# Causal maxima masked on VectorE, products made in sets, and a new order for all engines: a two-attention, expert-FFN kernel on one Trainium2 core

## What is computed

```python
_OFFSETS = list(range(41)) + [128, 96, 384]
idx = jnp.arange(T)[:, None] - deltas[None, :]        # A: each row looks at 44 earlier rows
k_mod = k_g * (1.0 + scale_embed)
scores = jnp.einsum('bhtd,bhtjd->bhtj', q, k_mod) * scale
scores = scores + pos_bias.T[None, :, None, :]
scores = jnp.where(valid[None, None], scores, jnp.finfo(scores.dtype).min)
attn = jax.nn.softmax(scores, axis=-1)
...
scores = jnp.einsum('bhqd,bhkd->bhqk', Q, K) / jnp.sqrt(jnp.float32(D_HEAD))   # B: causal attention
scores = jnp.where(causal, scores, -jnp.inf)
...
h = jax.nn.relu(jnp.einsum('nm,emh->enh', cont, We1) + be1[:, None, :])        # F: 8 experts, top 2
...
x = x + A(_layernorm(x)); x = x + F(_layernorm(x)); x = x + B(_layernorm(x)); x = x + F(_layernorm(x))
```

## Time and profile before

| | before |
|---|---|
| median of 3 runs | 1962.25 us (1960.55 to 1966.32) |
| the profiled execution: its time, its span | 1972.26 us, 1970.2 us |
| mean granted TensorE clock | 0.949 of full speed |
| busy PE, DVE, ACT, POOL | 1745.7, 1297.8, 804.7, 119.0 us |

### The profile page before, as it was taken

How to read it: one execution, slowest core, us unless ns; L and a number is a source line. 1 busy time by engine, 2 the same in 40 slices (tenths; PEclk the granted TensorE clock), 3 DMA queues, 4 the chain that set the end, 5 groups by cost and what they waited for, 6 DMA issues and landing times.

```text
span 1970.2 us, 29536 instructions
## 1 busy us (share of the span) xinstructions
PE 1745.7 (89%) x11263; PEld 918.3 (47%) x11312; DVE 1297.8 (66%) x3090; ACT 804.7 (41%) x1473; POOL 119.0 (6%) x155
## 2 busy tenths in 40 slices
PE   5588888899999899998999999998999899998976
PEld 2163454345453555436453455435554345454443
DVE  6939764785659756686659757696566964745433
ACT  1123425234453445434462434533454253452623
POOL 1010110001000100002000010001000010000000
PEclk9779988999999999999999999999999999998989
DMA  8220250014200250005200240003400023104000
GB/s 287 90 73 23 98 172 3 23 70 144 58 24 23 105 165 3 24 22 204 67 23 23 81 167 23 24 23 138 132 24 1 23 105 127 50 2 129 3 11 11
DMA packets 47842, 137.91 MB, mean 70 GB/s; under 512 B 6184, under 2 KB 18856, under 8 KB 42920
## 3 DMA queue, kind: packets, MB, share of 16 engines
q1 hardware_dynamic: 47704, 136.02, 21.1%
HBM read 80.79 MB, written 46.04 MB: 64 GB/s over the span
## 4 chain that ended last, share of the span: by engine, by line
PE 59%; DVE 28%; issue 5%; ACT 3%; DMA 3%; POOL 0%; SPq 0%; POOLq 0%; DVEq 0%; ACTq 0%
PE bank L1435 22%; DVE arena_AB L1216 15%; PE bank L1703 6%; PE bank L1718 5%; DVE arena_AB L1272 4%; PE bank L1606 4%; PE bank L1625 3%; PE bank L1523 3%; PE bank L1537 2%; PE bank L1590 2%; PE bank L1558 2%; PE bank L1456 2%; PE bank L1443 1%; PE bank L1608 1%; DMA arena_AB<-stacks 1%
## 5 line engine op out<-in xcount | busy, mean ns | idle before, releaser
L1216 DVE TENSOR_TENSOR arena_AB<-qT,kT 128x512 f32<-128x512 f32 x704 | 428.4, 683 | 8.6 <-ACT kT L971 7.6
L1435 PE MATMUL bank<-arena_F,kept 128*128 128x512 f32 (+1 forms) x544 | 265.3, 615 | 15.8 <-ACT cont_hi L1059 4.2
L1523 PE MATMUL bank<-arena_AB,slot_w 128*32 128x512 f32 x1408 | 212.4, 643 | 54.9 <-DVE arena_AB L1216 52.9
L1272 DVE TENSOR_REDUCE arena_AB<-bank 128x1 f32<-128x512 f32 (+3 forms) x512 | 214.5, 481 | 67.6 <-PE bank L1592 66.0
L1069 ACT ACTIVATE arena_F<-bank,kept 128x512 f32<-128x512 f32 x256 | 169.0, 691 | 152.0 <-PE bank L1435 149.6
L1034 ACT ACTIVATE arena_AB<-bank 128x512 f32<-128x512 f32 (+1 forms) x352 | 178.7, 577 | 105.9 <-PE bank L1608 105.6
L1435 PEld LDWEIGHTS bank<-arena_F,kept 128*128 128x128 f32 (+1 forms) x544 | 93.6, 190 | 124.0 <-issue 99.2
L1590 PE MATMUL bank<-arena_AB 96*128 96x512 bf16 (+3 forms) x512 | 132.9, 317 | 10.0 <-ACT arena_F L1069 3.3
L1606 PE MATMUL bank<-arena_AB 99*128 99x256 bf16 (+3 forms) x512 | 127.3, 305 | 3.2 <-DMA arena_AB<-maxima 3.0
L1703 PE MATMUL bank<-arena_F,kept 128*64 128x512 f32 x512 | 126.0, 613 | 3.0 <-issue 1.9
L1435 PE MATMUL bank<-xnT,kept 128*128 128x512 f32 x256 | 125.7, 630 | 2.1 <-ACT xnT L953 1.7
(11 more groups left out here) (192 smaller groups left out, 2493.7 us busy)
## 6 DMA issues: line engine op xcount, KB each, us to landing
arena_AB<-band SPq DMA_DIRECT2D x32, 1344.0 KB, 6.3
arena_AB<-stacks SPq DMA_DIRECT2D x64, 384.0 KB, 8.4
stacks<-arena_AB SPq DMA_DIRECT2D x48, 256.0 KB, 2.9
band<-arena_AB SPq DMA_DIRECT2D x32, 328.0 KB, 2.2
stacks<-xnT SPq DMA_DIRECT2D x32, 256.0 KB, 2.6
band<-kT SPq DMA_DIRECT2D x4, 1352.0 KB, 21.8
v<-V SPq DMA_DIRECT2D x8, 576.0 KB
stacks<-xn SPq DMA_DIRECT2D x16, 256.0 KB, 3.1
```

Source lines behind the costliest of these rows:

```text
L1216: nc.vector.tensor_tensor(prod[n % RD], qT[:, hf, :], kT[:, hf, at:at + T], ALU.mult).then_inc(sem["A"]["prod_made"], 1)
L1272: ins = nc.vector.tensor_reduce(neg_max[:, n, i:i + 1], ps[:, at:at + (i + 1) * P], AX, ALU.max, negate=True)
L1435: ins = nc.tensor.matmul(out(ps), w, x, start=n == 0, stop=n == len(pairs) - 1)
L1523: ins = nc.tensor.matmul(ps[HS * col:HS * (col + 1), :], slot_w[:, slot(n), :], prod[n % RD], start=False, stop=r == 3, skip_group_check=True)
```

## The change

Six edits.
1. B's maxima: the mask matmul L1592 is gone. VectorE takes the minimum of the negated masked scores in one call, `tensor_tensor_reduce`, which reads the scores in PSUM and a bf16 mask in SBUF, writes the scores' place in PSUM and gives the row value.
2. A's products: up to four offsets that lie 4 rows apart come from one instruction of 128x2048; the far offsets stay single. The ring of products holds 4 sets in place of 18 products.
3. A's `ahead` matmul moves from the front of a group to its end and covers 40, 24 or 384 columns in place of 512.
4. A's `oT`: the 16 matmuls of 128 keys stand first, and then the 16 of 40 keys.
5. Values are stored 17 columns a head and not 32.
6. The scheduler's lengths are new, each block's end has a delay after it, and a block on PE that changes the array's mode costs 0.1 more. The table has some 70 lengths; two lines of it are shown.

```diff
-        p.put(("S", h, n), ("PE", (0.3, 0.45, 0.25)[n], ("stack", h // 4, "DMA")), ("DVE", (0.62, 0.8, 0.36)[n]))
+        p.put(("S", h, n), ("PE", (0.22, 0.23, 0.12)[n], ("stack", h // 4, "DMA")), ("DVE", (0.62, 0.76, 0.37)[n]))
...
-            p.put(("oT", i), ("PE", 2.0, *needs), ("ACT", 0.55))
+            p.put(("oT", i), ("PE", 1.35 if i > 0 else 0.86, *needs), ("ACT", 0.48))
...
+AFTER = {"PE": 0.2, "DVE": 0.13, "ACT": 0.16, "POOL": 0.1, "SP": 0.0, "DMA": 0.0}
+LOAD = 0.1
...
+def tiled(u, phase):
+    kind = phase[0] if isinstance(phase, tuple) else phase
+    return kind in ("prod", "PV", "eo") or u.stage == "A" and kind == "oT"
...
-                if e != "DMA":
+                if e == "PE":
+                    t = max(t + LOAD, free[e] + (LOAD if tiled(u, x[1]) != last_tiled else 0.0))
+                elif e != "DMA":
                     t = max(t, free[e])
...
-            done[x] = t + blocks[x]
+        done[x] = t + blocks[x] + AFTER[e]
...
-        v_96 = sb("v_96", [P, TT, H, HS])
+        v_96 = sb("v_96", [P, TT, H * HV])
...
-                        for n in SETS[i]:
-                            at = PAD - SLOTS[slot(n)]
-                            if n >= RD:
-                                dve.wait_ge(*product_used(u, n - RD))
-                            nc.vector.tensor_tensor(prod[n % RD], qT[:, hf, :], kT[:, hf, at:at + T], ALU.mult
-                                                    ).then_inc(sem["A"]["prod_made"], 1)
+                        if i >= RQ:
+                            dve.wait_ge(*products_used(u, i - RQ))
+                        for run in runs(i):
+                            col, at, c = PRODUCTS[run[0]][2], PAD - SLOTS[slot(run[0])], len(run)
+                            k = kT[:, hf, at:at + T]
+                            k = bass.AP(k.tensor, k.offset, [k.ap[0], [4, c], [1, T]])
+                            ins = nc.vector.tensor_tensor(prod[i % RQ][:, col:col + c, :],
+                                                          qT[:, hf, :].unsqueeze(1).broadcast_to([P, c, T]), k, ALU.mult)
+                        ins.then_inc(sem["A"]["prod_made"], 1)
...
-                            ins = nc.vector.tensor_reduce(neg_max[:, n, i:i + 1], ps[:, at:at + (i + 1) * P], AX,
-                                                          ALU.max, negate=True)
+                            s = ps[:, at:at + (i + 1) * P]
+                            ins = nc.vector.tensor_tensor_reduce(
+                                out=s, in0=s, in1=causal[:, (TT - 1 - i) * P:T], scale=-1.0, scalar=BIG, op0=ALU.add,
+                                op1=ALU.min, accum_out=neg_max[:, n, i:i + 1])
...
+                            rows, cut = GROUP_J[g] * HPT, max(SLOTS[slot(n)] for k in SETS[i - 3:i + 1] for n in k)
+                            nc.tensor.matmul(ps[0:rows, 0:cut], is_slot[:, g * P:g * P + rows], ahead[:, 0:cut],
+                                             start=False, stop=True, skip_group_check=True).then_inc(full_, 1)
...
-                            for col in range(4 if i > 0 else 0):
+                        for g in range(4 if i > 0 else 0):
+                            for col in range(4):
...
-                        nc.tensor.matmul(ps[:, at:at + (i + 1) * P], q_st[0:K, h, i * P:(i + 1) * P],
-                                         k_st[0:K, h, 0:(i + 1) * P], start=True, stop=False, skip_group_check=True)
-                        ins = nc.tensor.matmul(ps[:, at + i * P:at + (i + 1) * P], ident_b[:], causal[:],
-                                               start=False, stop=True, skip_group_check=True)
+                        ins = nc.tensor.matmul(ps[:, at:at + (i + 1) * P], q_st[0:K, h, i * P:(i + 1) * P],
+                                               k_st[0:K, h, 0:(i + 1) * P], start=True, stop=True)
```

More of the change, by code:

```diff
@@ L13 @@
 HS = 32
+HV = HD + 1
+VW = H * HV + HS - HV
 HPT = P // HD
@@ L63, with slot, runs @@
 PRODUCTS = [(hf, g, col, r) for hf in range(2) for g in range(NG) for r in range(4) for col in range(GROUP_J[g] // 4)]
-FIRST = [hf * J + 16 * g for hf in range(2) for g in range(NG)]
-LAST = [n - 1 for n in FIRST[1:]] + [2 * J - 1]
-RD = 18
+RQ = 4
 SETS = [[n for n, p in enumerate(PRODUCTS) if (p[0], p[1], p[3]) == (hf, g, r)]
         for hf in range(2) for g in range(NG) for r in range(4)]
+def slot(n):
+    _, g, col, r = PRODUCTS[n]
+    return 16 * g + 4 * col + r
+def runs(q):
+    near = [n for n in SETS[q] if slot(n) < NEAR]
+    return [near] + [[n] for n in SETS[q] if slot(n) >= NEAR]
 QUADS = H // 4
@@ L144, in local_phases @@
         needs = [("qk", hf, "ACT"), ("qk", KD + hf, "ACT")]
-        needs.extend(("prod", k, "PE") for k in range(q) if of[-1] - RD in SETS[k])
-        p.put(("prod", q), ("DVE", 0.605 * len(of), *needs), ("PE", 1.3 if r == 0 else 0.95))
+        if q >= RQ:
+            needs.append(("prod", q - RQ, "PE"))
+        p.put(("prod", q), ("DVE", 0.067 * len(runs(q)) + 0.534 * len(of), *needs), ("PE", 0.86 if r < 3 else 1.12 if g == NG - 1 else 0.98))
         if r == 3:
-            p.put(("sT", hf * NG + g), ("ACT", 0.66, ("prod", q, "PE")))
+            p.put(("sT", hf * NG + g), ("ACT", 0.58, ("prod", q, "PE")))
         if q in between:
@@ L287, in setup_phases @@
     p.put("small", ("DVE", 3.0))
-    p.put("scaled", ("DVE", 4.0))
+    p.put("scaled", ("DVE", 1.4))
     p.put("split", ("DVE", 5.0))
@@ L609, in build @@
         xnT_ab = sb("xnT", [P, KD, T])
-        prod = [part(T, at=r * T) for r in range(10)]
+        prod = [part(4 * T, at=4 * r * T).rearrange("p (c t) -> p c t", c=4) for r in range(2)]
+        taken["AB"] = 10 * T
         band = part(2 * BW * H, at=0).rearrange("p (r s h) -> p r s h", r=2, s=BW)
@@ L613, in build @@
         sT = part(2 * NG * T).rearrange("p (g t) -> p g t", g=2 * NG)
-        prod.extend(part(T, at=taken["AB"] if r == 0 else None) for r in range(8))
-        assert len(prod) == RD
+        prod.extend(part(4 * T).rearrange("p (c t) -> p c t", c=4) for _ in range(2))
+        assert len(prod) == RQ
         p_nat = part(2 * J * H, at=sT_at + 2 * NG * T).rearrange("p (r j h) -> p r j h", r=2, j=J)
@@ L733, in covered, with products_used @@
             return [x for x in latest(u, others) if FILLS[u, x][0] != FILLS[u, name][0]]
-        def product_used(u, n):
-            if n in LAST:
-                return bank_full(u, ("sT", LAST.index(n)))
-            return nth(u, "prod_used", sum(k not in LAST for k in range(n + 1)))
+        def products_used(u, q):
+            if q % 4 == 3:
+                return bank_full(u, ("sT", q // 4))
+            return nth(u, "prod_used", q - q // 4 + 1)
         def step_done(u, n):
```

159 lines of the change are left out of this document (81 added, 78 removed).

## The result

The changed kernel takes 1979.97 us (median of four runs, 1979.49 to 1980.28), the kernel before 1963.17 beside it: ratio 1.0085, 95% interval 1.0067 to 1.0102. It is slower by 17 us (0.85%, clear of the noise), where I forecast 12 us faster (1950 for 1962). The profiled execution took 1979.71 us, its span is 1977.7.

What follows compares the result with a forecast made beforehand. TensorE was taken as the bound, busy 94% of a round, with VectorE setting some stretches. Terms -2 (front), +9 (four rounds) and -18 (end) gave -11: 1961 us profiled, median 1951, stated as 1950, range 1900 to 1985.

Steps and rivals of the forecast that it cites:

- in the first 586 us the expert stages move ahead into time that TensorE had free: Part ahead of the four rounds: moved expert work fits idle time, gains mostly eaten by waits; -2 us.
- The round: A4's round, costed stretch by stretch: 230.9 us in place of 226.3, mask savings handed back as waits for VectorE.
- the raw scores: B's raw scores, now standing alone: eight heads of 2.0 us set the pace; TensorE waits 7.0 us for 4.3.
- the bare sets: Last 13 product sets of A4, without expert work beside them: TensorE .86 a set, VectorE 2.2, so TensorE waits.
- the +9 for four rounds: The four equal rounds together: 9 us longer, since each is even or a few us longer.
- TensorE's savings: Whole program: TensorE has some 70 us less work from masks, `ahead`, `oT` and mode changes.
- The masks: B's raw scores: 512 mask matmuls at .06 us each spare TensorE 30.7 us.
- the first rival: TensorE stays the bound: VectorE's waits stay hidden, all 70 us arrive, 1892 to 1900 us; chance 20%.
- VectorE's total rises by 18: Whole program: accumulator reads at .095 us add 49 us to VectorE, fewer product instructions save 31.
- The rival of the slow read: B's maxima: the accumulator's read costs up to .22 us, adding 32 us, 1982 us; chance 31%.
- The rival of half rate: B's maxima: the minimum runs at half rate, adding 87 us, 2037 us; chance 4%.
- my two signs: Signs of a slower kernel: heads over 2.2 us, or tile 0's softmax held back by more than 6.3 us.

Runs made afterwards that it cites:

- e1: The changed kernel with the lengths and scheduler of before, so all new instructions in exactly the old order: 1929.0 us, ratio 0.9831.
- e7: The kernel before with only the matmuls of `oT` regrouped: 1947.0 us, ratio 0.9910.
- e4: The kernel before with only the masked minimum on VectorE in place of mask matmuls and plain maxima, old order: 1965.8 us, ratio 1.0018.
- e3: The changed kernel with the mask matmuls and plain maxima of before, in the new order: 1978.9 us, ratio 1.0081.
- e6: The changed kernel in the order of before, with the mask matmuls and plain maxima of before: 1922.1 us, ratio 0.9788.
- e2: The kernel before with the changed kernel's lengths, delays and charges, so the old instructions in the new order: 2016.7 us, ratio 1.0274.

## Why the prediction was wrong

**The direction.** Between the profiled executions I forecast -11 and it came out at +7.5: 18 us, of which the part ahead of A3 made 17 (+14.9 for -2), the rounds 3 (+11.8 for +9) and the end -1 (-19.2 for -18). The medians missed by 30 us (1980 for 1950). The 11 that are left are 10 for the distance between the profiled execution of before and its median, which I took to hold after the change too, and 1 for rounding 1951 down to 1950. All executions of the changed kernel lie within 1 us of each other (1979.5 to 1980.3), the profiled one among them.

**The step that failed** is "in the first 586 us the expert stages move ahead into time that TensorE had free". TensorE had idle time there (101 us in e1), but the moved work did not go into it: 24 us more of its work stand at the front (e1 beside the changed kernel), the front is 36 longer, and the idle time grew to 113. In the stretch from A1's products to A2's alone, 24.4 us of added work cost 26.6. I had seen the same work leave the end and booked -18 there, so I counted the gain and not its price. The 21 us that the new instructions bring at the front in the old order (565.0 for 586.2) went under in it.

**The round** came out near the forecast: 230.9 for 232.6 measured, and rounds of 228 to 233 and a last part near 448 were seen (231.8 to 232.6, and 447.1). VectorE's way from the first product to the softmax was 63.0, measured 64.6 (898.25 - 833.7); the latency to the weighing 12.0, measured 12.2; the rest 155.9, measured 155.8. The second half held the moved expert work as put. In part this was luck. In the raw scores the eight heads took 14.3 (969.50 to 983.83) and not 16.0, but what stands around them took 9.7 and not 7.3; and I read TensorE's work in that stretch before as 25 us where the window has 27.3, so that its wait there was 2.0 and not 4.3, and is 3.9 now and not 7.0. I also took the bare sets for the place where TensorE would wait. In the windows it waits 4.5 us in the products and 13.4 behind them, in the hole at the softmax, and the waits before L1555 are 62, up from 53, not "well over 100". And the +9 for four rounds hid how large both sides were: the new instructions alone take 27.6 off them (e1, 890.1 for 917.7), the order puts 39.4 on.

**TensorE's savings** were put at 70 and came to 58. `oT` was right (1.44, e7 17 of 19.7). The masks were not: without them TensorE's busy time is 19 us less in e4 (1726.6 for 1745.7), and 10 less in the changed kernel than in e3 (1687.5 for 1697.7), for a forecast of 30.7. The fall of the clock behind a wait in the raw scores explains this where I looked (e4, B3); elsewhere the cause is not shown. In time, e3, e4 and e6 show that the exchange brings nothing in either of those two orders, as my "what the masks release is handed back" has it; only the first rival had counted all of it as time.

**VectorE.** A call with its read costs .04 to .05 more than the plain maximum and not .095, so that "VectorE's total rises by 18" became a fall by 9: 33 us from the products, 24 back for the maxima (128 heads of 1.79 for 1.60). The rival of the slow read is false, and the kernel was slower all the same. The rival of half rate is false too: passes of 512 and 128 columns start .65 and .25 before their successors, 1.04 ns a column.
By the Trainium skill's rule on instructions that may be held (VectorE: DVE Perf Modes, "Two Vector instructions with no wait between them") neither the read nor the next pass is held here, since all operands start in the same quadrant of partitions. The trace agrees: the pass that starts at 971.27 is .73 long, and the read and the next pass both start at 971.92, before it ends.

**The rival that came nearest** is none of those I named. I had the order only inside a round's net of +4.6, and no rival in which the order alone costs 50 (e1 and e2). I gave the slower side its chance for a reason that the runs refute: of my two signs for it the first did not come (heads of over 2.2 us; they are 1.79), and the second came by .3 us a round (6.6 for the 6.3 between the last product and the softmax of tile 0).
